# The closing of a 32-group graph network kernel, written in another order on all five engines

## The chip, the cores and the metric

The kernel runs on one core of a Trainium2 chip. The metric is the device time of one launch in microseconds (us), as the median of three runs.

The core has TensorE (PE in the profile) for matmuls, VectorE (DVE), ScalarE (ACT), GpSimd (POOL) and SyncE (SP), which only issues DMAs here. Each engine works through its own list of instructions in the order in which they are written. An engine whose next instruction waits for a semaphore stands still, whatever is ready behind it.

## The reference

128 graphs of 128 nodes with 256 features pass through a graph attention block with a top-16 cut, and then through three layers of attention and feed-forward. Cut to what matters:

```python
h = relu(layernorm(x))
x = x + L0(h)            # attention over adj > 0, keep the 16 largest, times h @ W, elu
h = relu(layernorm(x))
for l in range(3):       # L1
    scores = si[:, :, None] + sj[:, None, :] + attn_b[l]
    scores = where(mask, leaky(scores), -inf)
    h1 = layernorm(h + softmax(scores) @ h, g1[l], beta1[l])
    ff = gelu(h1 @ W1[l] + b1[l]) @ W2[l] + b2[l]      # 256 -> 1024 -> 256
    h = layernorm(h1 + ff, g2[l], beta2[l])
return x + h
```

## The kernel before

**Groups and units.** Four graphs make one group, so there are NG = 32 groups. A unit (k, l) is layer l of group k: its attention (128x128 scores for each graph), a layer norm, and the feed-forward with its 1024 hidden features cut into eight chunks m = 0 to 7. The units run in the order of 3k + 4l, so that layers of neighbouring groups are interleaved. The last units are (NG-1, 0), (NG-2, 1), (NG-3, 2), (NG-1, 1), (NG-2, 2) and (NG-1, 2). Between the last two there is no other group's layer left, and behind (NG-1, 2) there is nothing.

**The steps of a unit.** Names are those of the helpers in the code; letters in brackets are the engines.
- `node_scores` [DVE, L2268] forms the two node sums. `turn_sj` [PE, L3078] spreads one of them, `leaky` [ACT, L1120], `scores_mask` and `scores_max` [DVE], `exps` [ACT, L1131], `turn_p` [PE, L3088], `p_copy` [ACT, L1141], `agg` halves 0 and 1 [PE, L3100] and `y1_sum` halves 0 and 1 [DVE, L2311] follow each other. `agg` half 1 writes the PSUM bank that `y1_sum` half 0 reads, so it waits for it.
- `y1_moments` [DVE, L2111 and L2116], `h_coefs` [POOL, L444 to L449] and `h_norm` [ACT, L1083] are the first layer norm. `turn_h`, `ht_high` and `ht_low` [PE L3112, ACT L1149, DVE L2327], once for each half d, turn it and split it in a high and a low part. `h_scale` and `h_bias` [POOL, L486 and L496] form the residual in H.
- Chunk m: `mm1` [PE, L3042 to L3044, 6 matmuls], `gelu` [ACT, L1069], `a_high` [ACT, L1077], `a_low` [DVE L2336 for odd m, POOL L506 for even m], `mm2` [PE, L3065 to L3067, 12 matmuls]. `mm1` of a chunk waits for the `gelu` two chunks before it, and `gelu` waits for the `mm2` three chunks before it. Both count over the border of units.
- `y_sum` and `y_moments` [DVE, L2346], `y_coefs` [POOL], `y_norm` [ACT, L1083], `y_scale` and `y_bias` [POOL, L513 and L523 or L530] are the second layer norm. It makes the input of layer l + 1 (X), or the output of the group, which `add_out` [POOL, L539] adds in DRAM by a DMA. `mm2` chunk 0 of the next unit waits for `y_sum`. `h_scale` of a layer 2 unit waits until the DMA of the group before has landed.

**The first block** of a group (L0) runs beside this: `turn_e0`, `z_leaky`, `z_mask`, `z_max`, `z_exps`, `z_topk`, `turn_z`, `z_copy`, `z_mix`, `mix_high`, `mix_low`, `z_agg`, `z_out`, `elu_exp`, `elu`.

**What sets the order.** Each engine's block has three functions that are written out by hand, line by line: `opening`, `iteration(i)`, which runs for groups 5 to 26, and `closing`, the last five groups. Nothing sorts them at build time. ACT uses one table for Gelu and another for Exp, and the program has an ACT_TABLE_LOAD at every change between the two.

Of the kernel before, what the change touches and what calls it, by code (L numbers as in the profile page):

```python
# [16 lines left out]
NG = B // G  # L17
# [110 lines left out]
def build_program(nc, x, adj, W0, a0, attn_w, attn_b, W1, b1, W2, b2, g1, be1, g2, be2, out):  # L128
    ctx = ExitStack()
    with ctx:  # L130
# [128 lines left out]
        def _(sp):  # L259
# [137 lines left out]
            def closing():  # L397
                park_mask(NG - 3)
                load_adj(NG - 2)
                load_mask(NG - 4, 0)  # L400
                load_mask(NG - 5, 1)
                load_mask(NG - 6, 2)
                store_x1(NG - 4)
                load_mask(NG - 3, 0)
                park_mask(NG - 2)
                load_mask(NG - 4, 1)
                load_x(NG - 1)
                store_x1(NG - 3)
                load_adj(NG - 1)
                load_mask(NG - 5, 2)  # L410
                load_mask(NG - 2, 0)
                park_mask(NG - 1)
                load_mask(NG - 3, 1)
                store_x1(NG - 2)
                load_mask(NG - 4, 2)
# [3 lines left out]
                store_x1(NG - 1)  # L419
                load_mask(NG - 1, 1)  # L420
                load_mask(NG - 2, 2)
# [8 lines left out]
        def _(pool):  # L430
# [404 lines left out]
            def closing():  # L835
                a_low(NG - 5, 1, 2)
                y_scale(NG - 4, 0, 0)
                y_scale(NG - 4, 0, 1)
                y_bias(NG - 7, 2, 1)
                y_bias(NG - 4, 0, 0)  # L840
                y_bias(NG - 4, 0, 1)
                a_low(NG - 5, 1, 4)
                add_out(NG - 7)
                a_low(NG - 5, 1, 6)
                h_scale(NG - 6, 2, 0)
                h_bias(NG - 5, 1, 1)
                a_low(NG - 6, 2, 0)
                h_scale(NG - 6, 2, 1)
                h_coefs(NG - 3, 0)
                y_coefs(NG - 5, 1)  # L850
                a_low(NG - 6, 2, 2)
                y_scale(NG - 5, 1, 0)
                y_scale(NG - 5, 1, 1)
                y_bias(NG - 5, 1, 0)
                y_bias(NG - 5, 1, 1)
                a_low(NG - 6, 2, 4)
                h_coefs(NG - 4, 1)
                x_coefs(NG - 1)
                a_low(NG - 6, 2, 6)
                h_bias(NG - 6, 2, 0)  # L860
                h_bias(NG - 6, 2, 1)
                h_scale(NG - 3, 0, 0)
                h_scale(NG - 3, 0, 1)
                h_bias(NG - 3, 0, 0)
                h_bias(NG - 3, 0, 1)
                a_low(NG - 3, 0, 0)
                h_scale(NG - 4, 1, 0)
                a_low(NG - 3, 0, 2)
                r_coefs(NG - 2)
                a_low(NG - 3, 0, 4)  # L870
                h_scale(NG - 4, 1, 1)
                y_coefs(NG - 6, 2)
                y_scale(NG - 6, 2, 0)
                y_scale(NG - 6, 2, 1)
                a_low(NG - 3, 0, 6)
                h_coefs(NG - 5, 2)
                a_low(NG - 4, 1, 0)
                h_bias(NG - 4, 1, 0)
                y_bias(NG - 6, 2, 0)
                y_coefs(NG - 3, 0)  # L880
                a_low(NG - 4, 1, 2)
                y_bias(NG - 6, 2, 1)
# [3126 lines left out]
```

## Time and profile before

| | before |
|---|---|
| median of 3 runs | 2841.56 us (2840.77 to 2841.84) |
| span of the profiled execution | 2840.5 us |
| PE matmul busy | 2719.1 us, 96% |
| ACT busy | 2326.9 us, 82% |
| DVE busy | 2293.8 us, 81% |
| POOL busy | 2080.0 us, 73% |
| mean granted TensorE clock | 0.979 |

The span runs from the first to the last instruction; the 1.1 us between it and the median lie around it. PE is the engine with the largest share. A share over the whole span says little about the closing, which on PE is the last 515 us, so it is read in stretches. In the waits, "PE ps_ff L3065 <- DVE H L2346" means that PE's matmul of line 3065 stood for that time until DVE's instruction of line 2346 was done.

### The profile page before, as it was taken

To read this page: it belongs to the slowest core of one execution; us is meant where nothing else is said; L and a number is where in the kernel's file an instruction comes from. 1 tells how busy PE (TensorE), PEld (TensorE's weight loads), DVE (VectorE), ACT (ScalarE), POOL (GpSimd) and SP (SyncE) were. 2 spreads that over 40 slices of the span, in tenths; PEclk is the share of its full clock that TensorE was granted. 3 is DMA by queue.
4 is the path that set the end of the run, shared out by engine and by line. 5 is a ranking of instruction groups with operands and counts; after the bars stand their busy time and mean duration, and the time that the engine had idled before them with its cause. 6 is when DMAs were issued, how large, how long until landed. Compare 5 with 4: busy or idle time off the path is not lost.

```text
span 2840.5 us, 55392 instructions
## 1 busy us (share of the span) xinstructions
PE 2719.1 (96%) x17764; PEld 2449.2 (86%) x17764; DVE 2293.8 (81%) x7766; ACT 2326.9 (82%) x4806; POOL 2080.0 (73%) x2217
## 2 busy tenths in 40 slices
PE   4698999999999999999999999999999999999995
PEld 4578988999999998998899899999899999888884
DVE  6777888888888888888888888888888888887542
ACT  4577988888888888888888888888888888888763
POOL 0355777877777787787787777778777777877774
PEclk8798999999999999999999999999999999999997
DMA  5000010111011011101101110110111011010001
GB/s 182 25 27 27 29 33 11 32 35 35 27 34 35 9 34 35 35 27 35 35 9 35 35 35 27 35 34 9 35 35 34 27 35 27 19 25 20 11 10 15
DMA packets 96322, 88.63 MB, mean 31 GB/s; under 512 B 9120, under 2 KB 94368, under 8 KB 96032
## 3 DMA queue, kind: packets, MB, share of 16 engines
q1 hardware_dynamic: 79136, 68.32, 7.8%
q0 software_dynamic: 16896, 16.78, 4.6%
q8 instruction: 141, 2.31, 0.3%
q14 instruction: 149, 1.22, 0.2%
HBM read 47.34 MB, written 37.75 MB: 30 GB/s over the span
## 4 chain that ended last, share of the span: by engine, by line
PE 80%; POOL 5%; issue 5%; DVE 4%; ACT 3%; DMA 2%; POOLq 0%; SPq 0%; ACTq 0%; DVEq 0%
PE ps_ff L3065 11%; PE ps_mm L3042 11%; PE ps_mm L3044 11%; PE ps_mm L3043 10%; PE ps_ff L3066 10%; PE ps_ff L3067 10%; PE ps_ag L3100 5%; PE ps_ht L3112 3%; PE ps L3164 2%; DMA out<-H 2%; POOL a_lo L506 2%; PE ps_s L3088 1%; PE ps_s L3078 1%; PE ps L3177 1%; PE ps L3178 1%
## 5 line engine op out<-in xcount | busy, mean ns | idle before, releaser
L3065 PE MATMUL ps_ff<-w_hi,a_hi 128*128 128x256 f32 x3072 | 892.0, 290 | 10.1 <-POOL a_lo L506 5.3
L506 POOL TENSOR_TENSOR a_lo<-A,a_hi 128x512 fp32r<-128x512 f32 x384 | 524.3, 1366 | 486.7 <-ACT a_hi L1077 486.4
L3066 PE MATMUL ps_ff<-w_lo,a_hi 128*128 128x256 f32 x3072 | 855.6, 279 | 0.0
L3067 PE MATMUL ps_ff<-w_hi,a_lo 128*128 128x256 f32 x3072 | 855.0, 278 | 0.0
L1069 ACT ACTIVATE A<-ps_mm,b_col 128x512 f32<-128x512 f32 x768 | 517.3, 685 | 251.7 <-PE ps_ff L3067 147.8
L3042 PE MATMUL ps_mm<-ht_hi,w_hi 128*128 128x512 f32 x1536 | 627.0, 408 | 3.7 <-DVE ht_lo L2327 2.8
L3065 PEld LDWEIGHTS ps_ff<-w_hi,a_hi 128*128 128x128 f32 x3072 | 578.2, 188 | 45.7 <-issue 11.7
L3044 PE MATMUL ps_mm<-ht_lo,w_hi 128*128 128x512 f32 x1536 | 606.5, 395 | 0.0
L3043 PE MATMUL ps_mm<-ht_hi,w_lo 128*128 128x512 f32 x1536 | 604.6, 394 | 0.0
L3066 PEld LDWEIGHTS ps_ff<-w_lo,a_hi 128*128 128x128 f32 x3072 | 579.0, 188 | 12.5
L3067 PEld LDWEIGHTS ps_ff<-w_hi,a_lo 128*128 128x128 f32 x3072 | 579.2, 189 | 0.0
L2336 DVE TENSOR_TENSOR a_lo<-A,a_hi 128x512 fp32r<-128x512 f32 x384 | 386.0, 1005 | 135.7 <-ACT a_hi L1077 134.5
L1077 ACT ACTIVATE a_hi<-A 128x512 fp32r<-128x512 f32 x768 | 465.9, 629 | 4.7
L3044 PEld LDWEIGHTS ps_mm<-ht_lo,w_hi 128*128 128x128 f32 x1536 | 289.7, 189 | 63.1
L3042 PEld LDWEIGHTS ps_mm<-ht_hi,w_hi 128*128 128x128 f32 x1536 | 290.3, 189 | 53.7 <-ACT A L1069 8.1
L3043 PEld LDWEIGHTS ps_mm<-ht_hi,w_lo 128*128 128x128 f32 x1536 | 290.8, 189 | 42.8
L2268 DVE CUSTOM_DVE_ANT_0 junk<-X,wij_row 128x256 bf16<-128x256 f32 x768 | 281.8, 430 | 43.1 <-POOL X L530 33.9
L513 POOL TENSOR_TENSOR H<-H,g_row 128x512 f32<-128x512 f32 x192 | 265.3, 1395 | 47.8 <-ACT H L1083 47.6
L486 POOL TENSOR_TENSOR H<-X,g_row 128x512 f32<-128x512 f32 x192 | 268.8, 1402 | 22.5 <-DMA out<-H 19.9
L496 POOL TENSOR_TENSOR H<-H,bb_row 128x512 f32<-128x512 f32 x192 | 274.0, 1430 | 2.0 <-DVE bb_row L2099 1.6
L1083 ACT ACTIVATE H<-H,st_y_nmr,st_y_rstd 128x256 f32<-128x256 f32 x384 | 199.3, 592 | 53.4 <-POOL st_y_nmr L449 53.1
L2327 DVE TENSOR_TENSOR ht_lo<-ps_ht,ht_hi 128x512 fp32r<-128x512 f32 x192 | 131.3, 684 | 110.8 <-ACT ht_hi L1149 110.5
(120 smaller groups left out, 5315.2 us busy)
## 6 DMA issues: line engine op xcount, KB each, us to landing
xr<-in_x SPq DMA_DIRECT2D x32, 512.0 KB, 4.2
out<-x SPq DMA_DIRECT2D x32, 512.0 KB, 4.8
out<-H POOLq DMA_DIRECT2D x32, 512.0 KB, 6.2
mask_in<-mask_park SPq DMA_DIRECT2D x96, 128.0 KB, 4.1
adj_sb<-in_adj SPq DMA_DIRECT2D x32, 256.0 KB, 4.4
mask_park<-mask_out SPq DMA_DIRECT2D x32, 128.0 KB, 4.0
X<-in_L_gnn_W SPq DMA_DIRECT2D x3, 1024.0 KB, 5.2
H<-in_L_gnn_W SPq DMA_DIRECT2D x3, 1024.0 KB, 7.1
```

The lines of the kernel that those rows point to most:

```text
L496: pool.tensor_tensor(H[:, l, two], H[:, l, two], bb_row[:, l:l + 1, :].to_broadcast([P, 2, D]), ALU.add).then_inc(s_res[l], 1)
L506: pool.tensor_tensor(a_lo[:, at], A[:, at], a_hi[:, at].bitcast(F32), ALU.subtract).then_inc(s["a_lo_gpsimd"], 1)
L1069: act.activation(A[:, a_at(k, l, m)], ps_mm[m % 2][:], ACT.Gelu, bias=b1_col[:, l, m:m + 1]).then_inc(s["gelu_made"], 1)
L1077: act.activation(a_hi[:, at], A[:, at], ACT.Copy).then_inc(s["a_hi_made"], 1)
L2268: last = dve.tensor_tensor_reduce(out=junk[:, 2 * g + j], in0=X[:, l, g], in1=wij_row[:, l, j], scale=1.0, scalar=0.0, op0=ALU.mult, op1=A ...
L2336: tt(a_lo[:, at], A[:, at], a_hi[:, at].bitcast(F32), ALU.subtract).then_inc(s["a_lo_vector"], 1)
L3042: pe.matmul(ps_mm[m % 2][:], w1_hi[:, l, d, cols], ht_hi[:, ht_at(k, l), d], start=(d == 0), stop=False)
L3043: pe.matmul(ps_mm[m % 2][:], w1_lo[:, l, d, cols], ht_hi[:, ht_at(k, l), d], start=False, stop=False)
L3044: last = pe.matmul(ps_mm[m % 2][:], w1_hi[:, l, d, cols], ht_lo[:, ht_at(k, l), d], start=False, stop=(d == DC - 1))
L3065: pe.matmul(out_g, a_hi[:, at, cols], w2_hi[:, l, m], start=first, stop=False, skip_group_check=True)
L3066: pe.matmul(out_g, a_hi[:, at, cols], w2_lo[:, l, m], start=False, stop=False, skip_group_check=True)
L3067: last = pe.matmul(out_g, a_lo[:, at, cols], w2_hi[:, l, m], start=False, stop=final, skip_group_check=True)
```

## The change

Only the five `closing` functions differ. On each engine they hold the same calls with the same arguments as before (25 on SP, 205 on POOL, 441 on ACT, 293 on DVE, 394 on PE), each exactly once, and the order of the units on PE is the same. Nothing is added or taken out, and `opening`, `iteration` and the helpers are untouched. PE's list, at the border between units (NG-1, 1) and (NG-2, 2), is the one place where the diff is shown:

```diff
                 turn_h(NG - 2, 2, 0)
-                mm1(NG - 1, 1, 5)
-                mm1(NG - 1, 1, 6)
+                mm2(NG - 1, 1, 6)
                 turn_h(NG - 2, 2, 1)
-                mm2(NG - 1, 1, 2)
-                mm2(NG - 1, 1, 3)
-                mm1(NG - 1, 1, 7)
-                mm2(NG - 1, 1, 4)
+                mm2(NG - 1, 1, 7)
                 mm1(NG - 2, 2, 0)
-                mm2(NG - 1, 1, 5)
-                mm2(NG - 1, 1, 6)
-                mm2(NG - 1, 1, 7)
                 mm1(NG - 2, 2, 1)
```

Chunk 0 of (NG-2, 2) stood ahead of the last three mm2 of (NG-1, 1) and stands behind all of them now.

DVE's list from the last a_low of (NG-2, 2) on; ps_ag is read by y1_sum of (NG-1, 2), and the `H<-ps_ff,H` is y_sum of (NG-2, 2). Before:

```order
L2336 TENSOR_TENSOR a_lo<-A,a_hi 128x512
L2301 RECIPROCAL a_rden<-a_den 128x4
L2346 TENSOR_TENSOR H<-ps_ff,H 128x512 x2
L2111 BN_STATS st_y_six<-H 128x6 x4
L2116 BN_AGGR st_y_mv<-st_y_six 128x2 x4
L2311 SCALAR_TENSOR_TENSOR X<-ps_ag,a_rden,X 128x256 x4
L2111 BN_STATS st_h_six<-X 128x6 x4
L2116 BN_AGGR st_h_mv<-st_h_six 128x2 x4
L2327 TENSOR_TENSOR ht_lo<-ps_ht,ht_hi 128x512 x2
```

Now:

```order
L2301 RECIPROCAL a_rden<-a_den 128x4
L2311 SCALAR_TENSOR_TENSOR X<-ps_ag,a_rden,X 128x256 x4
L2111 BN_STATS st_h_six<-X 128x6 x4
L2116 BN_AGGR st_h_mv<-st_h_six 128x2 x4
L2346 TENSOR_TENSOR H<-ps_ff,H 128x512 x2
L2111 BN_STATS st_y_six<-H 128x6 x4
L2116 BN_AGGR st_y_mv<-st_y_six 128x2 x4
L2327 TENSOR_TENSOR ht_lo<-ps_ht,ht_hi 128x512 x2
```

The sum and moments of (NG-2, 2) moved from ahead of y1_sum of (NG-1, 2) to behind its moments, and the last a_low of (NG-2, 2) moved up, ahead of scores_mask. In the same list a_low(NG-2, 2, 5) moved ahead of node_scores(NG-1, 2).

ACT's list from the last gelus of (NG-2, 2) to the first ones of (NG-1, 2). Before:

```order
L1069 ACTIVATE A<-ps_mm,b_col 128x512 x2
L1120 ACTIVATE U<-ps_s,sib 128x128 x4
L1077 ACTIVATE a_hi<-A 128x512 x2
L1131 ACT_TABLE_LOAD
L1131 ACTIVATE U,a_den<-U,a_nmax 128x128 x4
L1141 ACTIVATE pt<-ps_s 128x512
L1083 ACTIVATE H<-H,st_y_nmr,st_y_rstd 128x256 x4
L1083 ACTIVATE X<-X,st_h_nmr,st_h_rstd 128x256 x4
L1149 ACTIVATE ht_hi<-ps_ht 128x512 x2
L1069 ACT_TABLE_LOAD
L1069 ACTIVATE A<-ps_mm,b_col 128x512 x2
```

Now:

```order
L1069 ACTIVATE A<-ps_mm,b_col 128x512
L1077 ACTIVATE a_hi<-A 128x512
L1120 ACTIVATE U<-ps_s,sib 128x128 x4
L1131 ACT_TABLE_LOAD
L1131 ACTIVATE U,a_den<-U,a_nmax 128x128 x4
L1141 ACTIVATE pt<-ps_s 128x512
L1083 ACTIVATE X<-X,st_h_nmr,st_h_rstd 128x256 x4
L1149 ACTIVATE ht_hi<-ps_ht 128x512 x2
L1083 ACTIVATE H<-H,st_y_nmr,st_y_rstd 128x256 x4
L1069 ACT_TABLE_LOAD
L1069 ACTIVATE A<-ps_mm,b_col 128x512
```

The last two a_high of (NG-2, 2) stand ahead of leaky now instead of behind it, and y_norm of (NG-2, 2), the row that writes H, moved from ahead of h_norm to behind the second ht_high.

POOL's list behind y_coefs of (NG-2, 2). Before:

```order
L539 DMA out<-H 128x4x256
L486 TENSOR_TENSOR H<-X,g_row 128x512
L496 TENSOR_TENSOR H<-H,bb_row 128x512
L506 TENSOR_TENSOR a_lo<-A,a_hi 128x512
L486 TENSOR_TENSOR H<-X,g_row 128x512
L496 TENSOR_TENSOR H<-H,bb_row 128x512
L506 TENSOR_TENSOR a_lo<-A,a_hi 128x512 x3
```

Now:

```order
L506 TENSOR_TENSOR a_lo<-A,a_hi 128x512
L523 TENSOR_TENSOR H<-H,be_row 128x512
L539 DMA out<-H 128x4x256
L506 TENSOR_TENSOR a_lo<-A,a_hi 128x512 x2
L486 TENSOR_TENSOR H<-X,g_row 128x512
L496 TENSOR_TENSOR H<-H,bb_row 128x512
L506 TENSOR_TENSOR a_lo<-A,a_hi 128x512
L486 TENSOR_TENSOR H<-X,g_row 128x512
L496 TENSOR_TENSOR H<-H,bb_row 128x512
```

The residual of the last unit (H<-X,g_row and H<-H,bb_row) moved from ahead of its a_low to between and behind them, and h_coefs of (NG-1, 2) stands ahead of y_coefs of (NG-2, 2) now.

## Rows read from the trace of the kernel before

**Rows 1.** The page: busy time of each engine, share of the span.
```profile
PE 2719.1 (96%) x17764; PEld 2449.2 (86%) x17764; DVE 2293.8 (81%) x7766; ACT 2326.9 (82%) x4806; POOL 2080.0 (73%) x2217
```

**Rows 2.** Busy time by stretch: PE, PEld, DVE, ACT, POOL, granted clock, DMA.
```profile
2325.00:2692.00 367.00, 363.17 (x2388) 326.83 (x2388) 278.58 (x937) 304.80 (x618) 284.34 (x302) 1.00 0.10 23
2692.00:2756.00 64.00, 59.54 (x388) 52.87 (x387) 34.05 (x107) 44.17 (x87) 43.87 (x45) 1.00 0.14 20
2756.00:2792.00 36.00, 24.82 (x156) 21.36 (x155) 18.24 (x63) 19.27 (x40) 21.77 (x26) 0.91 0.00 1
2792.00:2841.00 49.00, 26.68 (x152) 23.00 (x150) 7.22 (x16) 14.33 (x23) 22.43 (x21) 0.74 0.16 22
```

**Rows 3.** PE's waits from 2330 to 2680 us: total, times, longest.
```profile
PE ps_ff L3065 <- DVE H L2346: 1.6, 2, 1.1
PE ps_mm L3042 <- DVE ht_lo L2327: 0.7, 1, 0.7
```

**Rows 4.** PE's waits from 2756 to 2780 us, and from 2780 on.
```profile
PE ps_ff L3065 <- POOL a_lo L506: 1.2, 1, 1.2
...
PE ps_ht L3112 <- ACT X L1083: 6.8, 1, 6.8
PE ps_ag L3100 <- DVE X L2311: 1.9, 1, 1.9
```

**Rows 5.** Timeline of PE: start, duration, instruction, idle time before it.
```profile
2755.80 0.39 PE L3042 MATMUL ps_mm<-ht_hi,w_hi 128*128 128x512 f32 x1
...
2769.53 0.39 PE L3042 MATMUL ps_mm<-ht_hi,w_hi 128*128 128x512 f32 x1
...
2772.80 0.65 PE L3078 MATMUL ps_s<-ident,sij 128*128 128x128 f32 x4 [0.35 <-DVE sij L2268]
...
2780.69 1.13 PE L3100 MATMUL ps_ag<-X,pt 128*128 128x256 f32 x4 [0.69 <-ACT pt L1141]
2783.72 1.10 PE L3100 MATMUL ps_ag<-X,pt 128*128 128x256 f32 x4 [1.90 <-DVE X L2311]
```

**Rows 6.** Timeline of ACT, last two units.
```profile
2773.49 1.14 ACT L1120 ACTIVATE U<-ps_s,sib 128x128 f32<-128x128 f32 x4 [0.25 <-PE ps_s L3078]
2774.50 1.16 ACT L1077 ACTIVATE a_hi<-A 128x512 fp32r<-128x512 f32 x2
2775.69 1.28 ACT L1131 ACT_TABLE_LOAD   x1
...
2780.04 0.60 ACT L1141 ACTIVATE pt<-ps_s 128x512 f32<-128x512 f32 x1 [1.40 <-PE ps_s L3088]
...
2789.49 2.08 ACT L1083 ACTIVATE X<-X,st_h_nmr,st_h_rstd 128x256 f32<-128x256 f32 x4 [2.76 <-POOL st_h_nmr L449]
...
2795.36 0.60 ACT L1149 ACTIVATE ht_hi<-ps_ht 128x512 fp32r<-128x512 f32 x1 [1.99 <-PE ps_ht L3112]
2795.97 1.28 ACT L1069 ACT_TABLE_LOAD   x1
2799.70 0.69 ACT L1069 ACTIVATE A<-ps_mm,b_col 128x512 f32<-128x512 f32 x1 [2.44 <-PE ps_mm L3044]
```

**Rows 7.** Timeline of DVE, the same units.
```profile
2778.67 0.18 DVE L2301 RECIPROCAL a_rden<-a_den 128x4 f32<-128x4 f32 x1 [1.62 <-ACT U L1131]
2779.67 1.29 DVE L2346 TENSOR_TENSOR H<-ps_ff,H 128x512 f32<-128x512 f32 x2 [0.82 <-PE ps_ff L3067]
...
2782.43 0.38 DVE L2116 BATCH_NORM_AGGREGATE st_y_mv<-st_y_six 128x2 f32<-128x6 f32 x4
2782.73 0.84 DVE L2311 SCALAR_TENSOR_TENSOR X<-ps_ag,a_rden,X 128x256 f32<-128x256 f32 x2
```

**Rows 8.** Timeline of POOL: the last bias of (NG-1, 1), an a_lo, and the last unit.
```profile
2766.22 2.55 POOL L530 TENSOR_TENSOR X<-H,be_row 128x512 f32<-128x512 f32 x2
2768.73 1.30 POOL L506 TENSOR_TENSOR a_lo<-A,a_hi 128x512 fp32r<-128x512 f32 x1
...
2801.22 1.26 POOL L486 TENSOR_TENSOR H<-X,g_row 128x512 f32<-128x512 f32 x1 [4.85 <-DMA out<-H]
```

More of the change, by code:

```diff
@@ L1757, in closing @@
-                y_norm(NG - 4, 0)
-                h_norm(NG - 6, 2)
-                ht_high(NG - 6, 2, 0)
                 gelu(NG - 5, 1, 4)
@@ L1943, in closing @@
+                a_high(NG - 4, 2, 5)
+                p_copy(NG - 2, 1)
+                ht_high(NG - 1, 0, 1)
+                gelu(NG - 4, 2, 6)
+                a_high(NG - 4, 2, 6)
+                y_norm(NG - 3, 1)
                 gelu(NG - 4, 2, 7)
-                leaky(NG - 3, 2)
-                a_high(NG - 4, 2, 6)
-                ht_high(NG - 1, 0, 1)
-                h_norm(NG - 2, 1)
+                gelu(NG - 1, 0, 0)
                 a_high(NG - 4, 2, 7)
-                exps(NG - 3, 2)
@@ L2757, in closing @@
+                a_low(NG - 6, 1, 5)
+                y1_sum(NG - 4, 0, 0)
+                node_scores(NG - 5, 1)
+                z_topk(NG - 3)
+                a_low(NG - 6, 1, 7)
                 scores_mask(NG - 5, 1)
-                a_low(NG - 6, 1, 7)
+                scores_max(NG - 5, 1)
+                y_sum(NG - 6, 1)
                 y1_sum(NG - 4, 0, 1)
-                scores_max(NG - 5, 1)
-                y1_moments(NG - 4, 0)
-                y_sum(NG - 6, 1)
-                y_moments(NG - 6, 1)
@@ L2817, in closing @@
+                y1_sum(NG - 3, 0, 1)
+                ht_low(NG - 6, 2, 1)
+                y1_moments(NG - 3, 0)
+                node_scores(NG - 4, 1)
+                a_low(NG - 5, 1, 7)
+                z_topk(NG - 2)
+                z_recip(NG - 2)
+                y_sum(NG - 5, 1)
+                a_low(NG - 6, 2, 1)
+                y_moments(NG - 5, 1)
+                ht_low(NG - 3, 0, 0)
                 scores_mask(NG - 4, 1)
+                a_low(NG - 6, 2, 3)
+                masks(NG - 1)
@@ L3720, in closing @@
+                z_agg(NG - 2, 0)
+                mm2(NG - 6, 2, 3)
+                turn_p(NG - 4, 1)
+                mm1(NG - 6, 2, 7)
+                agg(NG - 4, 1, 0)
+                mm2(NG - 6, 2, 4)
+                agg(NG - 4, 1, 1)
+                mm1(NG - 3, 0, 0)
+                mm1(NG - 3, 0, 1)
                 mm2(NG - 6, 2, 5)
                 mm2(NG - 6, 2, 6)
-                mm1(NG - 3, 0, 0)
+                mm1(NG - 3, 0, 2)
+                turn_sj(NG - 5, 2)
                 z_mix(NG - 2, 1)
```

1176 lines of the change are left out of this document (581 added, 595 removed).

## Prediction

> **What bounds the kernel now.** I read the busy shares first: PE is busy 96% of the span, ACT 82%, DVE 81%, POOL 73% [rows 1]. PE sets the time, and only PE's idle time can be won, since no instruction goes away. Then I cut the closing, on PE the last 515 us, into stretches [rows 2]. From 2325 to 2692 PE stands 367.00 - 363.17 = 3.8 us. From 2692 to 2756, where units (NG-1, 1) and (NG-2, 2) begin with few neighbours left, it stands 64.00 - 59.54 = 4.5 us. From 2756 to 2792 it stands 36.00 - 24.82 = 11.2 us and from 2792 on 49.00 - 26.68 = 22.3 us. The last two are the attention of the last unit, its feed-forward and its closing norm, a chain of steps with nothing beside it. There the view of the waits names PE's long ones: 6.8 us for ACT's h_norm and 1.9 us for DVE's y1_sum [rows 4], and the granted clock falls to a mean of 0.74 [rows 2]. From 2325 to 2692 the two largest waits are 1.6 us for y_sum and 0.7 us for ht_low [rows 3]. One more number is used throughout: chunk steps (mm1 or mm2) take 1.37 us each on PE when nothing is late, from ten of them between 2755.80 and 2769.53 [rows 5].
>
> The change only re-orders, so its worth is the idle that goes less the idle that comes. I take the closing in four parts.
>
> **Part A, 2325 to 2692.** The new order puts more PE work where PE waited. Ahead of mm2 chunk 0 of (NG-5, 2), which waits for y_sum, 4.5 us of PE work stand behind the unit before instead of 2.8, and ahead of that of (NG-4, 2) 4.5 instead of 3.1. Between the two turn_h and mm1 of the units there are up to 10 us in place of 1.4 to 5. So the 2.3 us of [rows 3] should go. But other distances shrink: turn_p and agg are parted by one chunk step or less in seven units of the closing now, in three before, and agg then waits for p_copy, which stands in ACT's list behind whole norms of 2.08 us and table loads of 1.28 us [rows 6]. I walked the first 80 us of the new order with the durations of the rows: agg of (NG-5, 1) comes 0.5 us too early for p_copy, z_agg half 0 of group NG-3 0.3 us too early for mix_low, and one mm2 0.3 us too early for POOL's 1.30 us a_lo [rows 8]. That is 1.1 us new idle in 80, and at that rate 4.6 x 1.1 = 5 in the stretch if nothing else improves; the other end is no new idle at all. I take the middle of what is left: 3.8 us before, about 3.4 after, a gain of **0.4**, with bounds from +3.8 (all goes) to -1.5 (new idle at the rate of those 80 us).
>
> **Part B, 2692 to 2756.** The 4.5 us of before lie in several short gaps, all between two units' chunks [rows 2]. In the new order turn_h of (NG-1, 1) stands before the last two mm2 of (NG-3, 2), and turn_p of (NG-2, 2) stands 11.5 us of work behind its turn_sj in place of 4.6, so these waits go. New ones, by the same walk: turn_sj of (NG-1, 1) behind node_scores 0.6; mm2 chunk 0 of (NG-3, 2) behind a_lo 0.4; mm1 chunk 5 behind exps, a table load of 1.28 and a gelu 0.5; agg half 0 behind y_norm (2.08) and p_copy 0.6; agg half 1, which now follows half 0 at once, behind y1_sum (0.84 and the hand-overs [rows 7]) 1.1; mm1 chunk 5 of (NG-1, 1) behind p_copy, a table load and a gelu 0.6. Together 3.8 against 4.5: a gain of **0.7**. The bounds are +4.5 (none of the new ones shows) and -2.1, if a second norm of 2.08 falls ahead of one of them and the rest stays as before.
>
> **Part C, from the end of (NG-1, 1) to the last attention.** The last unit's attention starts from y_sum of (NG-1, 1), so from its last mm2; and the only PE work beside that chain is unit (NG-2, 2). Before, one chunk of (NG-2, 2) stood ahead of that mm2; now none does, so the chain starts one chunk step, 1.37 us, earlier against the same total work. Of that some is given back:
> - a_low(NG-2, 2, 5) stands ahead of node_scores(NG-1, 2) now. Its gelu waits for mm2 chunk 2, which ends nine chunk steps, 9 x 1.37 = 12.3 us, behind the last mm2 of (NG-1, 1), so a_low ends at 14.3 to 14.5. Before, node_scores began when the bias was done, 2766.22 + 2.55 = 2768.8, 13.0 us behind 2755.80, and turn_sj at 17.0 [rows 5, 8]. Node sums of 3.1 to 4.2 us now end at 17.7 to 18.6. PE has thirteen chunk steps, work until 17.8. So turn_sj moves to about 18.1, 1.2 later.
> - leaky stands behind the last gelu and a_high on ACT (0.69 + 0.6), another 0.5 late. In exchange exps no longer waits behind two a_high (1.16) and the table load behind them: before, leaky ended at 2774.63 and exps could start only at 2775.69 + 1.28 = 2776.97, 2.3 us later; now the load runs beside scores_mask and scores_max, and exps starts 1.7 behind leaky [rows 6]. It ends 1.1 late. The 1.2 us wait of mm2 for POOL's a_lo [rows 4] goes, since that a_high no longer stands behind leaky, but this only makes PE wait later, in front of turn_p.
> - turn_p waited for PE's last mm2 before (0.8 us after exps was done at 2778.67) and now follows exps at once, so agg half 0 comes 0.4 late.
>
> Gain of C up to agg: 1.37 - 0.4 = **1.0**.
>
> **Part D, y1_sum of the last unit.** Before, DVE did y_sum and y_moments of (NG-2, 2) from 2779.67 to 2782.8, and y1_sum half 0 began at 2782.73 although agg half 0 was done at 2780.69 + 1.13 = 2781.82 [rows 5, 7]. Now y1_sum stands in front. Gain: 2782.73 - 2781.87 = **0.9**. Everything behind it up to h_norm and turn_h is one chain and comes earlier by it. What covers the moved step: y_sum and moments take 3.1 us, and DVE is free from the end of y1_moments until ht_low some 6 us later; y_coefs follows h_coefs on POOL. y_norm (2.08 us) now stands between ht_high and the table load ahead of the first gelu. Before, the load began at 2795.97 and the gelu at 2799.70, so ACT stood 2799.70 - 2795.97 - 1.28 = 2.45 us [rows 6]; 2.08 fits, with 0.4 us to spare.
>
> The trace shows the load as 1.28 us with the next instruction right behind it [rows 6]. The Trainium skill (ScalarE: Activation LUTs, What ACT_TABLE_LOAD costs) puts a switch at about 2.66 us, load and drain together. By that price, an estimate from that page, y_norm and switch would end 1.0 us after the gelu is due and D would lose all it gains; by the row nothing is lost. I go by the row.
>
> Behind it, the last unit's feed-forward runs at the same clock as before, since PE's long idle ahead of it (6.8 us) stays. The residual on POOL now comes behind a_low: the DMA of add_out delayed h_scale by 4.85 us before [rows 8], and the even a_low stood behind it, but PE never waited for them there, so nothing is won. y_sum of the last unit needs h_bias half 1, which by the walk ends 0.9 us before PE's last mm2: nothing lost. The closing norm and the last DMA are the same.
>
> **Sum.** 0.4 + 0.7 + 1.0 + 0.9 = 3.0 us. Against the profiled 2840.5 that is 2837.5, and with the 1.1 us around the span 2838.6; 2841.56 - 3.0 gives the same. I predict **2838.6 us**. A measurement tells about 0.2% from no change, here 5.7 us, so the forecast lies inside it.
>
> **Rivals.**
> - *The early idle really goes.* The walk of A and B may be too harsh: hand-over times of 0.1 us decide each of its small stalls, and most are 0.3 to 0.6 us. If A and B give 3.8 and 4.5 less one unavoidable 1.1 (agg half 1), they give 7.2, and with C and D the gain is 9.1: 2832.5. For it speaks that every wait of [rows 3] has its distance widened; against it the short turn_p to agg distances. To pass 5.7 us it needs 3.8 of the 7.2. Chance 0.23.
> - *p_copy becomes the wait (slower).* ACT's list holds a norm, an exps or elu_exp with its table load ahead of p_copy, and seven agg stand within one chunk step of turn_p. ACT is at 83% of the first stretch [rows 2], so it can hardly catch up. If ACT comes late by one more norm (2.08) at six of the seven, PE loses 12.5, less 3.0: 2851. It decides from five places on: 5 x 2.08 - 3.0 = 7.4. Against it: where I walked, the lateness was 0.5. Chance 0.10.
> - *Nothing moves but places.* The waits are those of a chain whose length is given, and C gives back all of its 1.37 (node_scores at 4.2 and not 3.1 us, as before, because POOL's a_lo runs beside it): A and B nil, D 0.9: 2840.7. Chance 0.12.
> - *The moved y_norm does not fit.* Now that work runs up to the load, the engine may have to empty itself first. If that takes as long as the load itself, 1.28 us [rows 6], less the 0.4 to spare, the first gelu is 0.9 late: 2839.5. Against it: ahead of exps the load followed a_high at once [rows 6]. Chance 0.05. [...]
> - The forecast case, gains of 1 to 5 us: 0.50.
>
> **How the numbers follow.** Faster by over 0.2% is the first rival: 0.23. Slower by over 0.2% is the second: 0.10. Within 0.2% are the others: 0.67. The range takes in A to D with A and B at their gaining bounds less a little, 2833.5, and on the other side A and B at their losing ends with C and D nil, 2841.56 + 1.5 + 2.1 = 2845.2, cut to 2844.0, since both ends at once are unlikely.
>
> **What would show it.** Right: PE's idle in the stretch up to the same amount of work as 2692 about 3 to 4 us, and PE waits for p_copy (ps_ag from ACT pt) new in the list; agg half 1 of (NG-1, 1) waiting about 1.1 us; DVE's y1_sum of the last unit within 0.1 us of agg's end; h_norm of the last unit ending 2.5 to 3 us earlier; y_norm, table load and gelu 0 on ACT in a row with a gap under 0.6 us. Wrong: h_norm of the last unit at 2791 or later; PE waits for ps_ag or ps_mm over 8 us in total (second rival); or PE idle under 1.5 us up to 2692 (first rival). From the first gelu of the last unit to the end both kernels should take the same time; if they do not, the walk of the last feed-forward is wrong.

## The result and the profile after

The changed kernel takes 2855.8 us (median of four runs, 2853.9 to 2858.0) where the kernel before took 2841.7 (2840.8 to 2844.7) beside it: a ratio of 1.0047, with a 95% interval of 1.0034 to 1.0061. It is 13 to 14 us **slower**; the forecast was 2838.6 and the range ended at 2844.0.

The span of the profiled execution is 2856.2 us, against 2840.5. On PE the closing begins with mm1(NG-5, 0, 4), at 2325.83 us before and 2328.03 after, so 2.2 us of the difference lie ahead of anything that was changed. From there to the end of the span it is 514.7 us before and 528.2 after. This length, "the closing" below, is the better measure, since what lies ahead of it differs by up to 5.4 us from run to run. Within it, kernels with the same order up to a point agree there within 1 us, except e8 below, which is 2.3 us late before its own edit. The busy shares (as [rows 1]):

```profile
PE 2723.8 (95%) x17764; PEld 2448.9 (86%) x17764; DVE 2303.2 (81%) x7766; ACT 2339.5 (82%) x4814; POOL 2081.1 (73%) x2217
```

The stretches, cut at nearly the same number of matmuls as [rows 2]: from the closing's start to 2692 of before, on to the last mm2 of (NG-1, 1), and the whole closing. Columns as in [rows 2], the granted clock third from the end. First the kernel before, then the changed one:

```profile
2325.83:2692.00 366.17, 362.34 (x2384) 326.13 (x2383) 277.75 (x936) 304.44 (x618) 284.34 (x302) 1.00 0.10 23
2325.83:2840.50 514.67, 473.37 (x3075) 423.35 (x3073) 337.27 (x1121) 382.21 (x768) 372.41 (x390) 0.97 0.11 21
```
```profile
2328.03:2709.10 381.07, 367.71 (x2386) 327.27 (x2385) 281.40 (x930) 317.43 (x627) 288.32 (x303) 0.99 0.11 24
2709.10:2772.00 62.90, 59.09 (x381) 51.36 (x380) 34.75 (x113) 43.08 (x85) 45.24 (x45) 1.00 0.08 12
2328.03:2856.20 528.17, 479.09 (x3075) 423.70 (x3073) 343.09 (x1121) 396.09 (x777) 375.62 (x390) 0.97 0.10 20
```

In the first stretch PE stands 381.07 - 367.71 = 13.4 us, where it stood 3.8. In the second it stands 3.8. Over the whole closing PE stands 49.1 us instead of 41.3, which is 7.8 of the 13.5 us. The other 5.7 us are PE's busy time, 479.09 instead of 473.37 for the same matmuls. The waits of PE in the first stretch (2325 to 2700 us; total, times, longest), which answer to [rows 3], name the largest single loss:

```profile
PE ps L3142 <- DVE e L2172: 7.3, 2, 7.2
PE ps_ff L3065 <- POOL a_lo L506: 2.2, 3, 1.1
PE ps_mm L3042 <- ACT A L1069: 1.9, 4, 0.8
PE ps_ff L3065 <- DVE a_lo L2336: 0.7, 2, 0.5
```

One wait of 7.2 us, for e0_scores of the last group, holds more than half of it. The timeline of DVE there (start, duration; the operations are eight of 128x256 f32, each with two operands in SBUF):

```profile
2526.92 0.41 DVE L2172 CUSTOM_DVE_ANT_0 kept<-hn,wa_row 128x256 bf16<-128x256 f32 x1
...
2527.26 1.50 DVE L2172 CUSTOM_DVE_ANT_0 U<-hn,wa_row 128x256 bf16<-128x256 f32 x1
...
2529.39 7.24 DVE L2172 CUSTOM_DVE_ANT_0 kept<-hn,wa_row 128x256 bf16<-128x256 f32 x1
...
2536.56 0.41 DVE L2172 CUSTOM_DVE_ANT_0 U<-hn,wa_row 128x256 bf16<-128x256 f32 x1
```

The same operation takes 0.41 us, 1.50 and once 7.24. e0_scores as a whole takes 10.8 us; before it took 2.85. What POOL did meanwhile (the same timeline, POOL):

```profile
2527.00 1.48 POOL L523 TENSOR_TENSOR H<-H,be_row 128x512 f32<-128x512 f32 x1
2528.84 1.34 POOL L539 DMA_DIRECT2D out<-H  x1 [0.36 <-POOL H L523]
2529.70 1.79 POOL L506 TENSOR_TENSOR a_lo<-A,a_hi 128x512 fp32r<-128x512 f32 x1
2530.93 2.99 POOL L513 TENSOR_TENSOR H<-H,g_row 128x512 f32<-128x512 f32 x2
2533.37 2.97 POOL L530 TENSOR_TENSOR X<-H,be_row 128x512 f32<-128x512 f32 x2
```

And PE, behind its wait:

```profile
2537.39 1.11 PE L3142 MATMUL ps<-ident,e 128*128 128x128 f32 x4 [7.17 <-DVE e L2172]
2538.29 1.06 PE L3112 MATMUL ps_ht<-ident,X 128*128 128x128 f32 x4
2539.15 1.91 PE L3100 MATMUL ps_ag<-X,pt 128*128 128x256 f32 x4
```

The long operation begins while POOL issues its own DMA, add_out(NG-6), and ends when POOL's last y_bias is done and POOL's queue stands still (2533.37 + 2.97 = 2536.34; 2529.39 + 7.24 = 2536.63). In the order before, that DMA stood behind the y_scale and y_bias, and e0_scores was over before they began. The wait costs more than its 7.17 us, since the clock falls in it. The stretch behind the wait has a granted clock of 0.57:

```profile
2537.40:2542.00 4.60, 4.60 (x20) 4.24 (x21) 1.77 (x6) 3.24 (x8) 0.14 (x1) 0.57 0.02 4
```

The agg above takes 1.91 us where it takes 1.10 at the full clock. The four steps from turn_e0 to the next mm1 take 5.1 us (2537.39 to 2542.51) instead of 3.2 in run e1 below (2525.27 to 2528.44), so with the wait the place costs some 9 us.

### The profile page after: what moved, and what is told of

It is laid out like the page before. It is cut to its first block, busy times and chain, and to the rows that moved or that the text cites. A ratio compares the mean times of both kernels' runs of the same rounds, so it can differ in the third digit from the quotient of the medians.

```text
span 2856.2 us, 55400 instructions
## 1 busy us (share of the span) xinstructions
PE 2723.8 (95%) x17764; PEld 2448.9 (86%) x17764; DVE 2303.2 (81%) x7766; ACT 2339.5 (82%) x4814; POOL 2081.1 (73%) x2217
## 4 chain that ended last, share of the span: by engine, by line
PE 69%; POOL 9%; issue 7%; DVE 6%; ACT 5%; DMA 3%; POOLq 0%; SPq 0%; ACTq 0%; DVEq 0%
PE ps_ff L3065 9%; PE ps_mm L3042 9%; PE ps_mm L3044 9%; PE ps_mm L3043 9%; PE ps_ff L3066 9%; PE ps_ff L3067 9%; PE ps_ag L3100 5%; DMA out<-H 3%; POOL a_lo L506 2%; PE ps_ht L3112 2%; POOL H L496 2%; PE ps L3164 2%; PE ps_s L3088 1%; DVE junk L2268 1%; POOL H L513 1%
```

## The experiments

Three theories stood at the start. **S**: POOL's run of operations starves the DVE operation; S1 says that POOL's DMA ahead of the run is needed for it, S2 that a long run alone does it. **D**: the DVE operation is slow by itself. Besides, the rest of the loss had to be placed: first or second half of the change, small waits, tail.

### e1: POOL held back

> The changed kernel with one wait more: POOL waits for DVE's e0_scores(NG-1) directly behind the DMA of add_out(NG-6), ahead of a_low(NG-4, 1, 2) and the two y_scale and y_bias of (NG-3, 0). Theory S (starved): in the changed kernel one operation of e0_scores took 7.24 us instead of 0.42 because POOL's operations, back to back behind the DMA, kept it from its operands. Then with POOL held back, e0_scores takes 2.8 to 4 us (10.76 in the changed kernel), PE's wait at turn_e0(NG-1) falls from 7.17 us to under 1, and the time falls by 6 to 9 us against the changed kernel, to 2847 to 2850 (x1.002 to x1.003 of the kernel before). POOL's y_scale of (NG-3, 0) come 1 to 4 us late and may cost up to 1 of it. Theory D (the DVE operation is slow by itself, by its data or its place on DVE): e0_scores still takes about 10 us, and the time stays at 2855 or rises.

```
@@ POOL, closing, changed kernel
                 add_out(NG - 6)
+                pool.wait_ge(s["e0_made"], NG)
                 a_low(NG - 4, 1, 2)
```

Measured: x1.0012 (1.0003 to 1.0021), by the ratios about 10 us less than the changed kernel's 1.0047, by the closings 7.4 (520.8 against 528.2). e0_scores takes 3.9 us, its slowest operation 1.50, and PE's wait is 0.24. The first line is the timeline of PE, the second the busy times of 2512 to 2532 us (columns as in [rows 2]):

```profile
2525.27 0.65 PE L3143 MATMUL ps<-ident,e 128*128 128x128 f32 x4 [0.24 <-DVE e L2173]
```
```profile
2512.00:2532.00 20.00, 19.15 (x115) 16.25 (x116) 15.79 (x66) 19.45 (x44) 15.85 (x16) 1.00 0.23 34
```

The clock stays at 1.00, and holding POOL cost PE nothing that shows. D falls; S stands. What is left is 3 us by the ratio and 6 by the closing:

```profile
2322.80:2843.60 520.80, 479.38 (x3075) 423.05 (x3073) 335.00 (x1121) 396.05 (x777) 377.07 (x390) 0.97 0.10 21
```

PE stands 520.80 - 479.38 = 41.4 us in it, as long as before (41.3). So none of these 6 us is recorded as waiting of PE. They are its busy time, 479.4 instead of 473.4 us. The profile can't show short waits of PE: a matmul is recorded as 0.39 us where the next one starts 0.23 us later, so a hand-over that is late by less than 0.16 us would lengthen the busy time only. That the new order has more of those is likely, but no run shows it.

### e2: the DMA behind the run

> The changed kernel with add_out(NG-6), POOL's DMA, moved behind the two y_scale and two y_bias of (NG-3, 0) instead of ahead of them; the same work otherwise. Theory S1 (the DMA issue ahead of the back-to-back operations is what starves the DVE operation): e0_scores takes 3 to 4 us, PE's wait at turn_e0(NG-1) is under 1 us, time 2847 to 2850. Theory S2 (any run of POOL operations back to back does it, DMA or not): one operation of e0_scores still takes 4 to 7 us, as long as the run of a_low, y_scale, y_scale, y_bias, y_bias lasts, and the time stays at 2853 to 2856. Theory D: 10 us and 2855, as in the changed kernel.

```
@@ POOL, closing, changed kernel
-                add_out(NG - 6)
                 a_low(NG - 4, 1, 2)
                 y_scale(NG - 3, 0, 0)
                 y_scale(NG - 3, 0, 1)
                 y_bias(NG - 3, 0, 0)
                 y_bias(NG - 3, 0, 1)
+                add_out(NG - 6)
```

Measured: x1.0034 (1.0022 to 1.0045). No operation of e0_scores is over 1.51 us, but four are at 1.5, so e0_scores takes 7.2 us and PE waits 3.45. Three of them in the timeline of DVE:

```profile
2521.77 1.51 DVE L2172 CUSTOM_DVE_ANT_0 U<-hn,wa_row 128x256 bf16<-128x256 f32 x1
...
2523.22 1.51 DVE L2172 CUSTOM_DVE_ANT_0 kept<-hn,wa_row 128x256 bf16<-128x256 f32 x1
...
2525.35 1.47 DVE L2172 CUSTOM_DVE_ANT_0 U<-hn,wa_row 128x256 bf16<-128x256 f32 x1
```

The one long hold is gone with the DMA, as S1 says; S2 expected 4 to 7 us in one operation. But the time I expected (2847 to 2850) did not come: without the DMA each DVE operation still waits for one POOL operation, and there is POOL work enough for four such waits. I had left that out. So the 10 us between e1 and the changed kernel have two parts: some 4 us for the DMA in front of the run (1.0047 against 1.0034; closings 528.2 and 524.2), and some 6 by the ratios, 3.4 by the closings, for e0_scores beside POOL's run at all. The intervals of e2 and the changed kernel overlap, so the first part rests on the trace more than on the times.

### e7 and e8: the same made in the kernel before

> The kernel before with e0_scores(NG-1) two steps later on DVE, behind a_low(NG-4, 1, 3), so that it runs from about 2521 beside POOL's y_bias, two y_scale, two y_bias and a_low, which stand back to back there without a DMA among them. The control of the next run. Theories S1: single operations of e0_scores take up to 1.5 us, as one POOL operation holds each, e0_scores as a whole 4 to 8 us, PE waits 2 to 5 us at turn_e0(NG-1). S2: one operation takes 5 us or more.

```
@@ DVE, closing, kernel before
-                e0_scores(NG - 1)
                 recip(NG - 2, 0)
                 a_low(NG - 4, 1, 3)
+                e0_scores(NG - 1)
```

> The same and, besides, add_out(NG-6), POOL's DMA, in front of the two y_scale and y_bias of (NG-3, 0) instead of behind them and a_low(NG-4, 1, 4). It makes in the kernel before what was found in the changed one. S1: one operation of e0_scores lasts until POOL's run ends, 5 to 7 us, PE's wait at turn_e0(NG-1) is 3 us longer than in the control, and the time 3 to 6 us more. S2 and D: no difference to the control of over 1 us.

```
@@ POOL, closing, kernel before, besides the edit of e7
                 y_bias(NG - 6, 2, 1)
+                add_out(NG - 6)
                 y_scale(NG - 3, 0, 0)
 ...
                 a_low(NG - 4, 1, 4)
-                add_out(NG - 6)
```

The control e7 takes x1.0023 (1.0013 to 1.0034): e0_scores 8.2 us, none of its operations over 1.51, PE waits 6.1, more than I had said. e8 takes x1.0033 (1.0022 to 1.0045), 3.1 us above e7 in the medians, though the two intervals overlap and e8 had lost 2 us more than e7 before its edit, 1.5 of them in a wait for y_sum. It has the long operation (timelines of DVE and of POOL in e8):

```profile
2522.46 6.38 DVE L2172 CUSTOM_DVE_ANT_0 U<-hn,wa_row 128x256 bf16<-128x256 f32 x1
```
```profile
2522.27 1.34 POOL L539 DMA_DIRECT2D out<-H  x1 [0.36 <-POOL H L523]
2523.13 3.00 POOL L513 TENSOR_TENSOR H<-H,g_row 128x512 f32<-128x512 f32 x2
2525.57 2.98 POOL L530 TENSOR_TENSOR X<-H,be_row 128x512 f32<-128x512 f32 x2
```

So two edits to the kernel before make the operation of 6.4 us that no kernel without that order of POOL shows. PE's wait is 1.7 us longer than in the control (7.8 against 6.1), not 3: single holds and one long hold cost nearly the same here, since POOL's run is the same. The trace settles the pair, the times do not. S1 is right on what makes the long operation. What costs PE is first that e0_scores runs beside POOL's SBUF work at all, and its place just ahead of turn_e0: two steps later on DVE cost 6.5 us by the ratio.

### e5 and e12: the operation by itself

> No part of the computation: out is a copy of x, to which POOL's DMAs add single tiles. Nine stages, run three times, in each of which DVE runs a stream of operations while POOL runs its own back to back, 128x512 f32 SBUF to SBUF like y_scale: (1) DVE's multiply-and-sum of e0_scores against 6 POOL operations, (2) the same with POOL's DMA ahead of them, (3) DMA and 3, (4) DMA and 12, (5) 12 without DMA, (6) DMA, a small 128x4 operation, 6, (7) DMA and 6 against a_lo's subtraction, (8) the same with one operand in PSUM, (9) DMA and 6 against bn_stats, one operand. Theory S1 (behind a DMA of its own POOL keeps the operands until its queue runs dry): in stages 2, 3 and 4 one DVE operation takes about 7 to 8 us, 3.5 to 4.5 us and 14 to 16 us, in stages 1 and 5 none over 2. Theory S2 (a long run of POOL operations does it alone): stages 1 and 5 show the same long operations as 2 and 4. Theory D (it was something else in that place): no DVE operation over 2 us in any stage. Stages 8 and 9 should show no hold at all, if it is about two operands in SBUF.

> No part of the computation, built like e5_bench: five stages, three times. DVE runs 32 multiply-and-sums of e0_scores, POOL its DMA and six operations back to back. (1) as stage 2 there: one DVE operation of 8.7 to 8.8 us. (2) POOL pauses behind the DMA until 8 operations of DVE are done: if the hold belongs to operations that follow the DMA at once, none over 1.5; if it stays until the queue has been empty, 7 to 9. (3) DVE starts when two of POOL's six are done: a hold of 4 x 1.75 - 0.1 = 7 us if the DMA still counts then, 1.5 if only operations pending during the DMA are held. (4) three operations, the DMA, three: operations of 1.5 before it and one of about 5 behind it. (5) each of POOL's operations waits for a semaphore of the one before: if a gap of 0.1 us frees the operands, none over 1.9 behind the first; if not, 8 to 10.

Both compute nothing of the reference. In e5, DVE's slowest operation of each stage, the same within 0.6 us in all three rounds:

| stage | slowest DVE operation, us |
|---|---|
| 6 POOL operations, no DMA; 12, no DMA | 1.47; 1.48 |
| DMA, 3 / 6 / 12 operations | 5.1 / 8.8 / 16.0 |
| DMA, small operation, 6 | 8.6 |
| DMA, 6, against a_lo's subtraction | 9.1 |
| DMA, 6, one operand in PSUM; bn_stats | no hold |

From the timeline of DVE, in the order of the stages:

```profile
63.47 1.47 DVE L208 CUSTOM_DVE_ANT_0 junk<-hn,row 128x256 bf16<-128x256 f32 x1
...
80.39 8.80 DVE L208 CUSTOM_DVE_ANT_0 junk<-hn,row 128x256 bf16<-128x256 f32 x1
...
100.42 5.10 DVE L208 CUSTOM_DVE_ANT_0 junk<-hn,row 128x256 bf16<-128x256 f32 x1
112.59 16.00 DVE L208 CUSTOM_DVE_ANT_0 junk<-hn,row 128x256 bf16<-128x256 f32 x1
...
218.47 9.65 DVE L227 TENSOR_TENSOR a_lo<-ps,a_hi 128x512 f32<-128x512 f32 x16
```

The hold grows by about 1.22 us for each POOL operation behind the DMA, which is their spacing then, and a hold over more than one of them does not exist without the DMA. The last line shows sixteen subtractions with one operand in PSUM, beside DMA and run: 0.6 us each, undisturbed. The Trainium skill (SBUF — State Buffer, Who interferes with whom) says that a DVE instruction with two SBUF inputs contends with a GpSimd instruction that reads SBUF, and that one with at most one, outside DVE's two-port performance modes, does not; the table agrees. The same page of the Trainium skill says that whoever comes first has the shared ports for the whole instruction, so for one instruction; the rows of 1.47 agree with it, those of 5.1, 8.8 and 16.0 do not, and the measurement decides.

e12 asks what ends the hold. As expected, a pause of POOL behind the DMA (until DVE has done eight operations) leaves none over 1.48 us. If DVE starts only when two of POOL's six are done, its first operation still takes 5.11, what is left of the run (I had said 7, by a wrong spacing). With the DMA in the middle of the run, operations before it take 1.47 and the one behind it 5.07. And if each POOL operation waits for a semaphore of the one before it, only the first hold is longer, 2.66 us, and the rest are 1.47. The timeline of DVE in stages 3, 4 and 5:

```profile
104.09 5.11 DVE L214 CUSTOM_DVE_ANT_0 junk<-hn,row 128x256 bf16<-128x256 f32 x1 [4.22 <-POOL Y L202]
...
124.97 5.07 DVE L214 CUSTOM_DVE_ANT_0 junk<-hn,row 128x256 bf16<-128x256 f32 x1
...
140.57 2.66 DVE L214 CUSTOM_DVE_ANT_0 junk<-hn,row 128x256 bf16<-128x256 f32 x1
143.16 1.47 DVE L214 CUSTOM_DVE_ANT_0 junk<-hn,row 128x256 bf16<-128x256 f32 x1
```

So both kinds of semaphore wait that were tried, a pause and a hand-over between two operations, end it. Why the DMA changes the behaviour is not shown.

### e3 and e6: the two halves

> On each engine the order of before up to about 2538 us of the run (on PE up to and without mm2(NG-4, 1, 7)), and the new order from there on. It leaves out the early half of the change, with the place where e0_scores(NG-1) is slow. The ledger of the two traces puts +17.1 us on the early half, 3.7 given back behind it while the other engines catch up, +4.4 between mm2(NG-1, 0, 0) and the end of (NG-3, 2), and -4.2 from there to the end. Theory E (the loss belongs to the early half, the rest is about neutral): 2839 to 2843, x0.999 to x1.0005. If the second half has a loss of its own of about 4 us, hidden in the changed kernel by the catching up: 2844 to 2847.

> The other half of run e3_only_second_half: the new order up to about 2538 us (PE up to and without mm2(NG-4, 1, 7)), the order of before from there on. If the halves add up, it takes what the changed kernel lost less what the second half alone costs (x1.0008): x1.0035 to x1.0045, 2852 to 2856, with e0_scores(NG-1) at about 10.8 us and PE's wait behind it at about 7 us. If the second half of the new order only costs something together with the first, it is x1.003 or less.

Both are cut on every engine at about 2538 us of before, on PE ahead of mm2(NG-4, 1, 7). e3 (the order before, then the new one) takes x1.0008 (0.9998 to 1.0017), e6 (new, then before) x1.0047 (1.0030 to 1.0064), with the operation of 7.24 us and PE's wait of 7.1 again. Its closing is 531.9 us, 3.7 more than the changed kernel's; the 1.2 us of the tail, which it lacks, are part of that. The loss belongs to the first half; the second alone is within the error of nothing. The closing of e3 is 517.0, of which 3.1 us stand as one wait of turn_p(NG-3, 1) at the seam, which neither order has.

### e11: do small waits add up?

> Run e1 (the changed kernel, POOL held until e0_scores is done) with two a_low one step earlier on POOL: a_low(NG-6, 2, 2) ahead of h_bias(NG-6, 2, 0) and a_low(NG-3, 0, 6) ahead of y_scale(NG-6, 2, 0). PE waited 1.12 and 0.90 us for these two in the changed kernel. Theory W (each small wait of PE costs its own length): both waits gone or under 0.2, the closing up to turn_e0(NG-1) 2.0 us shorter than in e1, and of that 1 to 2 us left at the end. Rival (the next engine is as late): the waits move to ACT's gelu or DVE's a_lo within the next two chunks and the closing is as long as in e1.

```
@@ POOL, closing, changed kernel, besides the edit of e1
-                h_bias(NG - 6, 2, 0)
                 a_low(NG - 6, 2, 2)
+                h_bias(NG - 6, 2, 0)
 ...
-                y_scale(NG - 6, 2, 0)
                 a_low(NG - 3, 0, 6)
+                y_scale(NG - 6, 2, 0)
```

Measured: x1.0012 (1.0002 to 1.0021), as e1; the closing 518.9 against 520.8, but turn_e0(NG-1) only 0.5 us earlier in it (202.0 against 202.5). PE's waits for POOL's a_lo fell from 1.6 to 0.2 us up to there, and others came up behind them (waits of PE from 2325 to 2690 us, three lines of nine):

```profile
PE ps_ff L3066 <- DVE a_lo L2337: 1.4, 2, 0.9
PE ps L3178 <- DVE mix_lo L2231: 0.9, 1, 0.9
...
PE ps_ff L3066 <- POOL a_lo L506: 0.2, 1, 0.2
```

mm2(NG-3, 0, 7) now waits 0.91 for DVE in place of mm2(NG-3, 0, 6)'s 0.90 for POOL, z_agg 0.92 in place of 0.24. The rival holds at this place: of 1.4 us of waits removed, 0.5 were left by turn_e0. That the end shows 1.9 is not explained by it. 1.5 of it lies behind the first gelu of the last unit, where the two orders are the same: PE's matmuls of mm1 follow each other at 0.43 us at first and at 0.23 later, and in e1 thirteen of them are slow, in e11 seven. This is where the clock comes back (in the kernel before the granted clock is 0.50 from 2797.80 to 2800.60 and 1.00 from 2803.20 on), and it differs from run to run (thirteen before, seven in e3, eight in e10).

### e4, e10 and e9: the tail

> The kernel before with parts C and D of the change alone: mm1(NG-2, 2, 0) moved behind mm2(NG-1, 1, 7) on PE and the new order of every engine from there to the end. The prediction gave C 1.0 and D 0.9 us; in the changed kernel the two together show 1.5. By the prediction 2839.8 (x0.9993), by the trace of the changed kernel 2840.2; with a wait that the new tail does not have there, 2841.7 or more.

e4 takes x0.9996 (0.9986 to 1.0005). Its second half gained 2.1 us behind mm1(NG-2, 2, 1), but PE lost most of one chunk step ahead of it. Without mm1(NG-2, 2, 0) in front of it, mm2(NG-1, 1, 6) stood and waited for its a_lo (timeline of PE):

```profile
2751.34 0.38 PE L3065 MATMUL ps_ff<-w_hi,a_hi 128*128 128x256 f32 x1 [1.34 <-POOL a_lo L506]
```

> Run e4 with two of its moves undone: mm1(NG-2, 2, 0) stays ahead of the last three mm2 of (NG-1, 1), where in e4 mm2 chunk 6 stood 1.34 us in its place, and node_scores(NG-1, 2) stays ahead of a_low(NG-2, 2, 5). e4 gained 2.1 us behind mm1(NG-2, 2, 1) and lost 1.5 ahead of it. If the moved mm1 is worth nothing by itself: turn_sj(NG-1, 2) about 2 us earlier behind the last mm2 of (NG-1, 1) than in e4 (17.0 instead of 19.0 us), and the time 2.5 to 3.5 us under the kernel before, x0.999. If node_scores is not what turn_sj waits for, or PE then waits for the last mm2 of (NG-2, 2) instead: as e4, x0.9996.

x0.9998 (0.9988 to 1.0008), closing 514.4, the shortest of all by 0.3. turn_sj(NG-1, 2) came at 18.6 us behind the last mm2 of (NG-1, 1), not at 17.0: node_scores started 0.7 later than before and took 5.3 us, beside POOL's a_lo and bias. Neither e4 nor e10 can be told from the kernel before, so no version here is shown to beat it.

> The kernel before with part D of the change alone: y_sum and y_moments of (NG-2, 2) behind y1_moments(NG-1, 2) on DVE, y_norm(NG-2, 2) behind ht_high(NG-1, 2, 1) on ACT, y_coefs behind h_coefs on POOL. By the prediction 0.9 us less: from agg half 0 to h_norm's end of the last unit 8.8 us instead of 9.7. In run e4 the last feed-forward was 0.7 us shorter besides (its second mm1 2.09 us instead of 2.76), since PE's idle time ahead of it was shorter; if that belongs to D it comes here too, and the gain in the trace is 1.6 us (x0.9994). The rival that the moved y_norm does not fit ahead of the table load: the first gelu 0.9 us late, no gain.

```
@@ kernel before; DVE, ACT and POOL, closing
-                y_sum(NG - 2, 2)
-                y_moments(NG - 2, 2)
                 y1_sum(NG - 1, 2, 0)
                 y1_sum(NG - 1, 2, 1)
                 y1_moments(NG - 1, 2)
+                y_sum(NG - 2, 2)
+                y_moments(NG - 2, 2)
 ...
-                y_norm(NG - 2, 2)
                 h_norm(NG - 1, 2)
                 ht_high(NG - 1, 2, 0)
                 ht_high(NG - 1, 2, 1)
+                y_norm(NG - 2, 2)
 ...
-                y_coefs(NG - 2, 2)
                 h_coefs(NG - 1, 2)
+                y_coefs(NG - 2, 2)
```

The surprise: x1.0034 (1.0021 to 1.0047), some 10 us slower (closing 525.0). The forecast gain is there: the first gelu of the last unit starts 42.98 us behind the last mm2 of (NG-1, 1) instead of 43.74, and fits. But y_norm(NG-2, 2) now ends at 2799.5, so POOL's y_scale, y_bias and the DMA of add_out(NG-2) come 8 us later against the same point, and in the order of POOL that this run keeps, a_low(NG-1, 2, 0) stands behind them. The timeline of POOL, and then of PE:

```profile
2799.59 1.28 POOL L513 TENSOR_TENSOR H<-H,g_row 128x512 f32<-128x512 f32 x1 [5.53 <-ACT H L1083]
...
2805.27 1.35 POOL L539 DMA_DIRECT2D out<-H  x1 [0.44 <-POOL H L523]
2811.67 1.25 POOL L486 TENSOR_TENSOR H<-X,g_row 128x512 f32<-128x512 f32 x1 [5.05 <-DMA out<-H]
2813.00 1.26 POOL L496 TENSOR_TENSOR H<-H,bb_row 128x512 f32<-128x512 f32 x1
2814.22 1.26 POOL L506 TENSOR_TENSOR a_lo<-A,a_hi 128x512 fp32r<-128x512 f32 x1
```
```profile
2815.63 0.55 PE L3065 MATMUL ps_ff<-w_hi,a_hi 128*128 128x256 f32 x1 [7.68 <-POOL a_lo L506]
```

The prediction had read this move of a_low ahead of add_out as "nothing is won". It wins nothing by itself, but it is what makes part D possible: without it D costs some 10 us instead of bringing 0.8.

## Why the prediction was wrong, point by point

**Part A, forecast +0.4, measured -14.9.** This is the step that failed: the stretch takes 381.1 instead of 366.2 us, 9.5 more of idle time and 5.4 more of busy time. I walked the new order with the durations of the rows of before, each fixed by its kind of instruction. But the duration of a DVE operation with two operands in SBUF depends on what stands in POOL's row beside it, 0.41, 1.5 or 7.24 us, and the change moved exactly that. Part C had allowed for it, with 3.1 to 4.2 us for node_scores; part A had not. No bound of mine held such a case: the longest hold of a DVE operation in the trace of before is about 1.2 us (an a_lo of 1.86 instead of 0.66), and I took neither it nor a multiple of it as a price. The event is worth about 10 us by the ratio of e1 and 7.4 by its closing (7.2 of wait, and the clock).

**A term put at nothing.** "PE sets the time, and only PE's idle time can be won, since no instruction goes away" left PE's busy time out of the sum. It grew by 5.7 us for the same matmuls. About 2 of them are the low clock behind the long wait; what the others are is open.

**The arithmetic of A.** 4.6 x 1.1 = 5 against 3.8 gives a lower bound of -1.3, where I wrote -1.5, and +0.4 is not the middle of +3.8 and -1.5, which is 1.2. With 1.2 the forecast is 2837.8, no nearer.

**The small waits of A.** Forecast for the first 80 us: 0.5 for p_copy, 0.3 for mix_low, 0.3 for an a_lo. Measured there: 0.5 and 0.8 for ACT's gelu (the second behind exps and its table load), 0.5 for DVE's a_lo, and two of 0.16; p_copy was in time every time. So the size was off by a factor of two and the names were wrong. Apart from the 7.17 us PE stood 6.2 us in the stretch, where I had 3.4. The two waits of [rows 3] for y_sum did go, as forecast, and so did the one for ht_low.

**Part B, forecast 3.8 us of idle.** Measured 62.90 - 59.09 = 3.8, with agg half 1 at 1.13 (forecast 1.1), mm2 chunk 0 of (NG-3, 2) at 0.57 (0.4), and turn_h and mm2 chunk 7, at 0.58 and 0.63, that I had not named. The sum is right, the parts half so.

**Part C, forecast +1.0, measured +0.4.** Of the 1.37 us, 0.94 was given back and not 0.4: agg half 0 starts 25.67 us behind the last mm2 of (NG-1, 1), before 24.73. node_scores began at 15.1 instead of 14.4, and took 4.2 us, the upper of my two values; with that turn_sj came at 19.1, and I had 18.1. The 1.37 itself is no sure gain: e4 shows that the moved mm1 covered a wait.

**Part D, forecast +0.9, measured +0.76.** y1_sum begins 0.11 us behind the end of agg, and y_norm, table load and gelu fit with 0.48 us to spare. The timelines of PE, DVE and ACT in the changed kernel:

```profile
2797.50 1.13 PE L3100 MATMUL ps_ag<-X,pt 128*128 128x256 f32 x4 [0.69 <-ACT pt L1141]
2799.76 1.10 PE L3100 MATMUL ps_ag<-X,pt 128*128 128x256 f32 x4 [1.13 <-DVE X L2311]
```
```profile
2798.74 0.88 DVE L2311 SCALAR_TENSOR_TENSOR X<-ps_ag,a_rden,X 128x256 f32<-128x256 f32 x2 [2.43 <-PE ps_ag L3100]
```
```profile
2811.90 2.06 ACT L1083 ACTIVATE H<-H,st_y_nmr,st_y_rstd 128x256 f32<-128x256 f32 x4
2813.98 1.28 ACT L1069 ACT_TABLE_LOAD   x1
2815.75 0.69 ACT L1069 ACTIVATE A<-ps_mm,b_col 128x512 f32<-128x512 f32 x1 [0.48 <-PE ps_mm L3044]
```

The load costs 1.28 us straight behind a norm, as the rows of before said. From the norm's end to the gelu's start 1.78 us pass, less than the 2.66 us that the prediction gives as the price of a switch, so the measurement decides against that price here. The rival that the moved y_norm does not fit is out. C and D together gave 1.2 us of 1.9. From the first gelu of the last unit to the end both kernels take nearly the same time, 40.8 us before and 40.5 now, as forecast.

**The rivals.** "p_copy becomes the wait" was the slower one, with 2851: the sign was right, the mechanism was not; there is no wait for p_copy in the first stretch at all. "The early idle goes" and "nothing moves but places" fail with part A.

**What stays open.** The closing of e1 is 6 us longer than that of before, its ratio says 3. Each closing is that of one profiled execution, and the times carry what lies ahead of it, so I can't say which is nearer. Why PE's busy time grew is open too. The last unit's second mm1 took from 1.6 us (e3) to 2.6 (before, e1), by where the clock comes back, so differences of about 1 us between two closings mean nothing.

## What to carry to other kernels

When instructions are moved, a walk with the old durations is not enough: check for each DVE operation with two SBUF operands which SBUF work of POOL will now stand beside it, and above all whether a DMA that POOL itself issues is followed by POOL operations without a wait between them. Such a run holds the DVE operation until it is over; here one wait on a semaphore, put behind the DMA, kept e0_scores and POOL's run apart and gave back 10 us of 13 by the ratios, 7.4 of 13.5 by the closings. Moving the DMA alone gave back some 4. And a move that wins nothing by itself may be the cover of another: take the parts of a change out one at a time before calling one of them free.

## What the runs showed of the hardware

- A DVE operation with two operands in SBUF that meets single POOL operations takes 1.47 instead of 0.41 us, each time; behind a DMA issued by POOL it takes as long as POOL's whole run: 5.1, 8.8 and 16.0 us for 3, 6 and 12 operations (e5). With one operand in PSUM, or one operand only, none of sixteen operations was held.
- The hold outlasts the DMA's issue (1.31 us): a DVE operation that first comes 3.9 us behind it is held too, for 5.11 us (e12). In both stages of e12 in which POOL waited for a semaphore behind the DMA the hold ended there: none over 1.48 us behind a pause, 2.66 and then 1.47 with a hand-over between operations.
- Within the hold POOL's operations follow each other at 1.22 us; when DVE gets its turn between them, at 1.40.
- After 7.2 us without matmuls PE worked 4.6 us at a granted clock of 0.57, near its lower level of 1.2 GHz; after 3.45 us (e2) turn_e0 took 0.74 instead of 0.65 us.
- The same matmuls in another order took 5.7 us more of PE's busy time (479.1 against 473.4 us in the closing), and 6.0 more in e1, whose idle time is that of before.
